# A graph network on one core: GpSimd multiplies gathered messages by their edge weights, and VectorE folds the step before ahead of adding the edge terms

## What is computed

```
m  = x @ W
xi = ew * m[dst];  xj = ew * m[src];  ea = ew * (edge_attr[:, :3] @ We + be)
h  = concatenate([xi, xj, ea]) @ Wpre + bpre
s1, s2 = segment_sum(h, dst), segment_sum(h * h, dst)
mn, mx = segment_min(h, dst), segment_max(h, dst)
```

## Time and profile before

| | us |
|---|---|
| median of 3 runs | 2921.49 (2921.08 to 2924.81) |
| span of the profiled execution | 3375.5 |
| DVE busy | 2090.7 (62%) |
| POOL busy | 1809.4 (54%) |
| PE busy | 1462.2 (43%) |
| ACT busy | 1242.7 (37%) |

### The profile page before, as it was taken

How to read it: one execution, slowest core, us unless ns; L and a number is a source line. 1 busy time by engine, 2 the same in 40 slices (tenths; PEclk the granted TensorE clock), 3 DMA queues, 4 the chain that set the end, 5 groups by cost and what they waited for, 6 DMA issues and landing times.

```text
span 3375.5 us, 29216 instructions
## 1 busy us (share of the span) xinstructions
PE 1462.2 (43%) x4582; PEld 639.7 (19%) x4583; DVE 2090.7 (62%) x3685; ACT 1242.7 (37%) x3273; POOL 1809.4 (54%) x1818
## 2 busy tenths in 40 slices
PE   3133444455434343334233344442323322477996
PEld 2011111111111111013011111110101100376553
DVE  5745567667645555666466677885655656743456
ACT  0022233333323332343255556554444445421122
POOL 3476666666666666660666666666666666111011
PEclk9995666666656655666555555555555555568986
DMA  5321222222222222220111122221111111116410
GB/s 126 76 50 47 50 49 51 49 50 49 53 49 54 51 47 53 53 54 16 39 47 49 49 51 51 59 53 47 49 41 47 47 24 24 37 60 206 135 66 6
DMA packets 124348, 186.68 MB, mean 55 GB/s; under 512 B 62045, under 2 KB 79154, under 8 KB 124127
## 3 DMA queue, kind: packets, MB, share of 16 engines
q0 software_dynamic: 57776, 89.59, 12.6%
q1 hardware_dynamic: 48894, 70.70, 6.8%
q10 hardware_dynamic: 17618, 25.71, 2.1%
HBM read 146.04 MB, written 39.84 MB: 55 GB/s over the span
## 4 chain that ended last, share of the span: by engine, by line
issue 25%; DVE 24%; PE 19%; DVEq 13%; ACT 10%; another core or an unknown queue 6%; ACTq 2%; POOL 1%; DMA 0%; POOLq 0%
ACT arena L1255 6%; PE mm L838 4%; DVE arena L1863 4%; PE mm L696 4%; DVE red L1877 3%; DVE red L1976 3%; PE hist L916 2%; PE l L987 2%; PE hist L778 2%; DVEq L1754 2%; DVEq L1876 2%; PE l L756 2%; DVE score L1843 2%; PE l L916 1%
## 5 line engine op out<-in xcount | busy, mean ns | idle before, releaser
L558 POOL DMA_INDIRECT arena<-b_tab,lin x815 | 813.7, 998 | 559.8 <-issue 344.3
L558 POOL DMA_INDIRECT arena<-kv_tab,rec x815 | 824.4, 1012 | 334.5 <-issue 299.1
L756 PE MATMUL l<-arena,identB 128*128 128x512 bf16 x996 | 395.1, 560 | 502.0 <-issue 265.1
L1255 ACT ACTIVATE arena<-arena,lin 128x64 f32<-128x64 f32 x1984 | 504.3, 334 | 213.0 <-issue 213.0
L838 PE MATMUL mm<-Wslots,eaT 48*128 48x512 f32 x248 | 234.2, 1097 | 684.5 <-ACT eaT L1249 320.3
L1976 DVE TENSOR_REDUCE red<-arena 128x128 f32<-128x2048 f32 x189 | 459.2, 2486 | 13.7 <-issue 12.8
L1863 DVE TENSOR_SCALAR arena<-arena,digit 128x512 bf16<-128x512 int16 x744 | 257.2, 414 | 97.4 <-issue 49.8
L756 PEld LDWEIGHTS l<-arena,identB 128*128 128x128 bf16 x996 | 115.3, 127 | 771.1 <-issue 456.0
L778 PE MATMUL hist<-arena,oh_lo 125*128 125x225 bf16 x400 | 170.7, 584 | 175.0 <-DVE arena L1834 142.8
L838 PEld LDWEIGHTS mm<-Wslots,eaT 48*128 48x128 f32 x248 | 72.2, 321 | 775.4 <-ACT eaT L1249 331.0
L1252 ACT ACTIVATE arena<-arena 128x1024 f32<-128x1024 f32 x62 | 65.5, 1057 | 394.0 <-DVE arena L1999 277.3
(11 more groups left out here) (380 smaller groups left out, 2445.5 us busy)
## 6 DMA issues: line engine op xcount, KB each, us to landing
arena<-at_tab SPq DMA_DIRECT2D x50, 800.0 KB, 4.5
at_tab<-T ACTq DMA_DIRECT2D x25, 800.0 KB
arena<-kv_tab,rec POOLq DMA_INDIRECT x815
arena<-b_tab,lin POOLq DMA_INDIRECT x815
at_pack<-arena SPq DMA_DIRECT2D x25, 256.0 KB
T<-at_pack SPq DMA_DIRECT2D x25, 256.0 KB
lin_tab<-lin ACTq DMA_DIRECT2D x62, 64.0 KB
lin<-lin_tab SPq DMA_DIRECT2D x62, 56.0 KB
```

The source lines that it names most:

```text
L558: return pool.indirect_dma_start(dst, None, table, offs(ap=index, axis=0))
L756: last = pe.matmul(l3[:, 0, :], identB[:], hot[:, j], start=False, stop=True, skip_group_check=True)
L1255: last = act.activation(dst[:, s], hh[u][:, s, 0:C], ACT.Identity, bias=bias[:, s:s + 1])
```

## The change

Four things change in the second loop.

- The multiplication by the edge weights leaves DVE and becomes one POOL instruction (`scale_rows`), of 128 partitions by 16 x 64 elements. The one for step g-1 stands in the stream of step g between its slots 5 and 6. It waits for `h_summed`, which DVE counts up in step g-1 right after L1987.
- DVE folds step g-1 (`add_step`) ahead of the edge term addition of step g, no longer behind it.
- DVE then waits for `h_scaled`, the end of POOL's multiplication, next to its wait for the edge term.
- POOL's first step and last step stand outside its loop, since the multiplication lags by a step.

```diff
@@ gpsimd, second loop
-            with aligned(pool, 0, pairs) as i:
-                for u in range(2):
-                    word = pool.value_load(stepW[0:1, bass.ds(2 * i + u, 1)], min_val=0, max_val=WMAX)
-                    left = word & 31
-                    pool.wait_ge(index_in[u], 16 * (i + 1))
-                    pool.wait_ge(LOOP1.free, 2 * i + u + 1)
-                    pool.sem_inc(pool_steps, 1)
-                    for s in range(SLOTS):
-                        with (pool.If(left >= s + 1) if s else nullcontext()):
-                            gather(G1[u][:, s], b_tab, row_of[u][:, s:s + 1]).then_inc(LOOP1.rows_landed[u], 16)
+            def scale_rows(u, done):
+                pool.wait_ge(h_summed, done)
+                h = hh[u][:, :, 0:C]
+                pool.tensor_tensor(h, h, bc(ewm[u], C), ALU.mult).then_inc(h_scaled, 1)
+
+            def gather_rows(g, u, turn, done, first=False):
+                word = pool.value_load(stepW[0:1, bass.ds(g, 1)], min_val=0, max_val=WMAX)
+                left = word & 31
+                pool.wait_ge(index_in[u], 16 * turn)
+                pool.wait_ge(LOOP1.free, done)
+                pool.sem_inc(pool_steps, 1)
+                for s in range(SLOTS):
+                    if s == 6 and not first:
+                        scale_rows(1 - u, done)
+                    with (pool.If(left >= s + 1) if s else nullcontext()):
+                        gather(G1[u][:, s], b_tab, row_of[u][:, s:s + 1]).then_inc(LOOP1.rows_landed[u], 16)
+
+            gather_rows(0, 0, 1, 1, first=True)
+            with aligned(pool, 1, pairs) as i:
+                gather_rows(2 * i - 1, 1, i, 2 * i)
+                gather_rows(2 * i, 0, i + 1, 2 * i + 1)
+            gather_rows(2 * pairs - 1, 1, pairs, 2 * pairs)
+            scale_rows(1, 2 * pairs + 1)
@@ vector, step1
                 prepare_step(2 * i + u + 1, 1 - u)
                 d().then_inc(LOOP1.free, 1)
-                tt(h, h, bc(ewm[u], C), ALU.mult)
+                dve.sem_inc(h_summed, 1)
                 tt(rel_hot[:], bc(relation[u], R), bm(relF[:], SLOTS), ALU.is_equal)
...
                 tt(v_, v_, rel_sum[:].unsqueeze(1), ALU.add)
+                add_step(2 * i + u, 1 - u)
                 dve.wait_ge(edge_terms, 2 * i + u + 1)
+                dve.wait_ge(h_scaled, 2 * i + u + 1)
                 tt(h, h, mm[:].rearrange("p a (s c) -> p (a s) c", c=C), ALU.add).then_inc(h_ready, 1)
...
-                add_step(2 * i + u, 1 - u)
                 end_step(u)
```

More of the change, by code:

```diff
@@ L321, in build @@
         h_ready, hmin_ready = sem("h_ready"), sem("hmin_ready")
+        h_summed, h_scaled = sem("h_summed"), sem("h_scaled")
         descents_found, descents_summed, unsorted_known = (
@@ L1963, in _ @@
             d().then_inc(hmin_ready, 1)
+            d().then_inc(h_summed, 1)
             d().then_inc(pack_split, 1)
```

## The result

The changed kernel takes 3044.18 us (median of 4 runs, 3042.31 to 3045.68), the kernel before 2922.72 us. The ratio is 1.041, with a 95% interval of 1.040 to 1.042. The forecast was 3060 us, slower. The profiled execution of the changed kernel has a span of 3044.0 us, as long as the timed ones, unlike the trace of before that the prediction had to work from.

The account below looks back on a forecast made before the run. DVE (16.9 us a step) or POOL's gathers were taken to bound the second loop's stretches. Slowest-of-ring, DVE and POOL terms 38 + 26 + 43 + 32 gave +139 us on the median: 3060 us, own range 3014 to 3115, 8-in-10 range 2970 to 3160.

Parts of the forecast that it names:

- The ring: Second loop: edge addition, ACT's square and copies, fold, next edge addition form a closed cycle of 18.2 us a step.
- the second and last stretch: Second-loop parts of 20 and 12 steps: 16.9 to 18.2 us a step, +26 us; 15.6 to 18.3, +32 us.
- GpSimd's multiplication: POOL's added multiplication in each second-loop step: 2.7 us, felt in full where POOL sets the pace; bounds 1.2 and 5.4 us.
- the last term: Final 12 steps of the second loop: 15.6 us a step rising to 18.3, set by POOL, +32 us.
- Idle times: Sign in the profile after: before most folds DVE idles about 4 us for ACT, in undisturbed steps.
- POOL's wait for `h_summed`: POOL, 6 gathers into a second-loop step, waits for L1987 of the step before: short, costed at nothing.
- The pauses: ACT's unexplained idle time before L1255, 213.0 us in 226 places of the profiled execution; taken as mostly absent from timed runs.
- the rival with covered waits: Timed second-loop steps have ACT's pauses, which cover the new costs; in half the steps 2990 us; chance 0.13.
- SP's queue: Index loads for step g+3 asked for behind ACT's end in step g, over a step early: no cost.
- The rival from busy time: Relieving DVE, the engine with highest occupancy, in the second loop gains up to 85 us, 2837 us; chance 0.07.

Follow-up runs that it names:

- the order alone: Kernel before with only the fold moved ahead of the edge term addition, DVE keeping the multiplication: 2989.9 us, ratio 1.021; on a chip with pauses 1.004.
- the idle multiplication: Kernel before plus one POOL multiplication per step whose result nobody reads or waits for: 3028.22 us, ratio 1.035; on a chip with pauses 0.972.
- the second trace of before: Kernel before, unchanged, profiled again on a chip where it runs without pauses: 2927.68 us, trace span 2925.9 us.
- the ring opened again: Changed kernel with the fold of h and its squares waiting only for ACT's square, not its masked copies: 3019.88 us, ratio 1.032.

## Why the prediction was right

**The ring.** Forecast at 18.2 us from one fold behind the loops; 18.1 us in the changed kernel, 18.03 us with the order alone. This step held in mechanism and size. The order alone costs 64 us. Forecast were 26 + 31 us from the second and last stretch; measured were 27 and 21 us there, and most of the rest behind the loop.

**GpSimd's multiplication.** The mechanism held: the stretches that GpSimd paces lose what it takes, as the idle multiplication shows. The size did not: that is the term that was mis-sized. I took 2.7 us, and it is 1.8 us in the stream. The two rows treat as many elements per partition, but are another operation, and a poor measure. The Trainium skill (GPSIMD Engine Reference, § 3.1) gives 4497 ns for 2048 elements, some 2.25 us here as an estimate; the trace has 1.91 us for the instruction, and the measurement decides. By 2.25 us the prediction's own terms are 31 + 26 + 36 + 31 = 125 us, some 15 us below its 139, not the 20 that it says.

**The ends of the loop.** The sum had no term for them. The ring has to be passed twice behind the last rows, 12.8 us. With 1.8 us the prediction's own sum is 14 x 1.8 + 26 + 16 x 1.8 + 12 x 2.6 = 111 us (the ring decides in the last stretch), and with the ends 124 us. Measured were 118 us between the two spans and 121 us between the medians. Stretch by stretch it is 25, 26, 29 and 31 us beside 22.6, 25.9, 33.8 and 24.2 us, so the last term was too large as well: POOL, and not the ring, paces most of that stretch. The forecast of 139 us came near in part by luck, since terms that were too large stood beside one that was missing.

**Gains and losses don't add.** The order costs 64 us and GpSimd 104 us, both together 121 us. A step takes the longest of the ring, POOL and DVE, not their sum. This is how the prediction formed each stretch.

**Idle times.** Forecast: about 4 us before most folds. Measured: 35 waits of 92.7 us, 2.6 us each. Where POOL paces, ACT was mostly ready, and in every second step of the ring DVE had the unpacking to do. POOL's wait for `h_summed` costs little, as forecast: 19.5 us in 8 waits, of which 9.5 us in the last one, behind the gathers.

**The pauses.** That the timed runs have none was inferred from 17.6 us a step. It held for the first timing: without pauses the two loops take 17.9 us a step on average. The agreement that the prediction found was loose, though. Its 17.6 us is an average over both loops, its 17.8 us is the second loop alone, which takes 17.3 us, and the part outside the loops is 739 us and not 769. The reason for the long trace was not the profiler, as one could have thought: on two chips each execution is that long. There the rival with covered waits is real for the order (ratio 1.004), and more: GpSimd's added work made the kernel faster. The changed kernel itself was not run on such a chip. The prediction put the loss down to ACT's idle time and SP's queue at no cost. In the undisturbed kernel the queue costs nearly nothing (POOL waits 6.2 us for indices in the changed one); with the pauses POOL waits 215 and 228 us for indices in the two traces of the kernel before, which is most of what the second loop loses. What makes ACT and other engines sit idle stays open. All that the traces show is that nothing the profile names ends this idle time, and that there is less of it ahead of ACT's copies in each kernel with a moved fold or with more work on POOL (132, 69 and 80 us, in place of 224).

**The rival from busy time.** DVE has the highest share, and moving work from it to GpSimd did not help. The Trainium skill (Perfetto Trace Analysis, § Identifying the Most-Contended Engine) would have started there. The trace here disagrees. In the second trace of before DVE waits for gathered rows ahead of L1987 in 40 of 62 steps, 137.8 us, and in the steps with few slots the new order closes a path that is longer by more than the instruction that was removed.

On the chip without pauses no run points to a version that beats the kernel before. With the ring opened again the change still loses 95 us, since GpSimd paces most steps and has become 1.8 us slower.

## What to carry to other kernels

Ask of each kind of step which engine sets its pace before moving work to the one that is less busy on average: here the receiver was the one that set the pace in two steps out of three. Take each engine's pace from a trace without such pauses, if there is one: here that moved GpSimd's in the second stretch from 15.3 to 15.9 us. When an operation is moved ahead of another within a loop step, follow the data once around: an order that lets one step of slack lie between producer and consumer may close into a ring, whose length is then the shortest a step can be. A row in which such a ring runs once, alone, gives its price.

## What was not expected of the hardware

- The kernel before takes 2923 to 2926 us on one chip and 3422 to 3434 us on two others, 17% more, with idle time ahead of ACT's copies that no semaphore explains, and with POOL waiting 227.5 us for row indices in place of 15.0 us. The same edit can win on the one and lose on the other: one idle multiplication per step gave 1.035 and 0.972.
- While GpSimd does a two-input multiplication in SBUF, some DVE instructions stand still until it is done: one of 0.42 us took 2.12 us, and the small comparison at L2010 2.05 us in place of 0.31 us, in the rows behind the loop. The folds' reductions weren't held (7.22 to 7.38 us). The Trainium skill (GPSIMD Engine Reference, § 1) says that the two engines share SBUF interfaces, in conflict with DVE instructions in a 2-port mode or with two SBUF inputs. For the comparison the trace agrees, since it has two inputs. The instruction that took 2.12 us has one input tensor; whether it ran in a 2-port mode no trace here shows.
